# Two-layer transformer kernel: GpSimd normalises each item's second head, one sum for queries and keys, weight loads on SyncE's queue, a first swap by TensorE

## The reference, cut to what matters

```python
def _rope(x, sin, cos):
    xe = x[..., ::2]
    xo = x[..., 1::2]
    re = xe * c - xo * s
    ro = xe * s + xo * c
    return jnp.stack((re, ro), axis=-1).reshape(x.shape)

def _attn(xq, ctx, wq, wkv, wo, bo):
    q = _heads(xq @ wq)
    k, v = jnp.split(ctx @ wkv, 2, axis=-1)
    ...
    q = _rope(q, sq, cq)
    k = _rope(k, sk, ck)
    sim = jnp.einsum('bhnd,bhmd->bhnm', q, k) * DH ** (-0.5)
    a = jax.nn.softmax(sim, axis=-1)
    o = jnp.einsum('bhnm,bhmd->bhnd', a, v)
    ...
    return o @ wo + bo
```

## Time and profile before

| | |
|---|---|
| Time, median of 3 runs | 410.18 us (409.72 to 411.91) |
| Profiled execution | 409.6 us, span 407.5 us |
| PE / DVE / ACT / POOL busy in the span | 93% / 79% / 73% / 38% |
| Share of the chain that ended last: PE, ACT, DVE, issue, POOL | 22%, 8%, 6%, 5%, 2% |

### The profile page before, as it was taken

The page is one execution under the profiler, slowest core; times in us unless marked ns, Lnnn a source line. Parts: engine busy times, 40 slices in busy tenths (PEclk is TensorE's granted clock), DMA queues, the critical chain, the costliest instruction groups (busy, mean ns, idle before and its releaser), DMA issues. The chain is left out here.

```text
span 407.5 us, 9917 instructions
## 1 busy us (share of the span) xinstructions
PE 380.4 (93%) x3600; PEld 286.3 (70%) x3600; DVE 321.4 (79%) x700; ACT 297.8 (73%) x1033; POOL 153.9 (38%) x145
## 2 busy tenths in 40 slices
PE   7689998999989999999999898989899999999997
PEld 3456676776767877777777667775777777787664
DVE  4799999889898898998898857764658878888740
ACT  2367687787786786887878894679579787987832
POOL 4565445442652432634244425330246530202010
PEclk9989999999999999999999999999999999999999
DMA  6234524323324122122221110000000000000001
GB/s 215 90 117 138 187 86 155 130 82 129 104 74 185 53 80 79 53 77 80 80 77 66 72 47 27 2 2 1 2 2 2 2 2 3 2 2 2 2 0 51
DMA packets 15970, 26.08 MB, mean 64 GB/s; under 512 B 3598, under 2 KB 5908, under 8 KB 15796
## 3 DMA queue, kind: packets, MB, share of 16 engines
q1 hardware_dynamic: 13588, 18.49, 12.7%
q0 software_dynamic: 1616, 5.97, 4.9%
q10 hardware_dynamic: 720, 1.00, 0.8%
HBM read 8.15 MB, written 0.52 MB: 21 GB/s over the span
## 5 line engine op out<-in xcount | busy, mean ns | idle before, releaser
L284 POOL TENSOR_TENSOR swp<-swp,small 128x512 f32<-128x512 f32 x64 | 82.2, 1297 | 121.5 <-PE bank L917 77.2
L411 ACT ACTIVATE prob<-bank,nmax 128x128 f32<-128x128 f32 x256 | 91.2, 390 | 4.1 <-DVE nmax L693 4.1
L506 ACT ACTIVATE raw<-bank,nmax 128x128 f32<-128x128 f32 x256 | 72.7, 390 | 13.7 <-DVE nmax L799 13.4
L411 ACT ACTIVATION_READ_ACCUMULATOR prob<-bank,nmax 128x1 f32 x256 | 59.1, 231 | 0.0
L799 DVE TENSOR_REDUCE nmax<-bank 128x4 f32<-128x512 f32 x64 | 41.2, 684 | 17.8 <-PE bank L917 17.8
L693 DVE TENSOR_REDUCE nmax<-bank 128x4 f32<-128x512 f32 x64 | 41.2, 685 | 16.9 <-PE bank L917 16.9
L917 PE MATMUL bank<-hT,wqkv 128*128 128x512 f32 x96 | 49.9, 606 | 1.1 <-ACT hT L393 1.1
L700 DVE TENSOR_TENSOR prob<-prob,rz 128x512 f32<-128x512 f32 x64 | 48.7, 762 | 2.2
L417 ACT ACTIVATE probT<-bank 128x512 f32<-128x512 f32 x32 | 19.1, 597 | 40.3 <-PE bank L1004 40.3
L239 POOL TENSOR_TENSOR rstd<-vare,neg_half 128x4 f32<-128x4 f32 x12 | 12.4, 1032 | 95.0 <-DVE vare L628 94.9
L1004 PEld LDWEIGHTS bank<-small,prob 128*128 128x128 f32 x256 | 28.8, 140 | 26.3 <-DVE prob L700 15.0
(11 more groups left out here) (113 smaller groups left out, 643.3 us busy)
## 6 DMA issues: line engine op xcount, KB each, us to landing
swp<-raw SPq DMA_DIRECT2D x128, 128.0 KB, 2.1
wqkv<-in_wqkv POOLq DMA_DIRECT2D x13, 256.0 KB, 3.4
wff<-in_wff POOLq DMA_DIRECT2D x1, 1024.0 KB, 5.9
wsq<-in_wsq POOLq DMA_DIRECT2D x1, 576.0 KB, 5.8
x<-in_x SPq DMA_DIRECT2D x2, 256.0 KB, 4.6
wqkv<-in_wqkv ACTq DMA_DIRECT2D x2, 256.0 KB, 6.0
wmod<-in_wmod POOLq DMA_DIRECT2D x1, 512.0 KB, 4.2
ctx<-in_ctx SPq DMA_DIRECT2D x1, 384.0 KB, 7.2
```

What stands on the lines that cost most here:

```text
L284: nc.gpsimd.tensor_tensor(four(swp[:, m % 2, f, :]), four(swp[:, m % 2, f, :]), sin[f], ALU.mult).then_inc(rope_sin[f], 1)
L411: last = nc.scalar.activation(prob[:, hh, bcols(u)], S[hh][:, bcols(u)], ACT.Exp, bias=nmax[:, s % 2, hh, u:u + 1], accum_out=zsum[:, s % ...
L506: last = nc.scalar.activation(prob1[:, s % 2, hh, bcols(u)], score_bank(s, hh)[:, bcols(u)], ACT.Exp, bias=nmax[:, s % 2, hh, u:u + 1])
```

## The change

Five things change in layer 0, and some places in layer 1 are moved.

1. The second head's multiplication by the inverted row sums moves from VectorE to GpSimd (`normalise_second`). VectorE still inverts the sums (`invert_sums`).
2. `rope_sum` adds queries and keys in one instruction of 1024 elements and stands ahead of `normalise`. Its semaphore `roped` is one for both.
3. The weight loads move from GpSimd's queue to SyncE's, behind `swap(m)`, after a wait for the next score; the three large ones are cut in pieces.
4. Item 0 is not swapped by DMA: TensorE multiplies by weights whose columns are swapped in pairs already (`wswap`, a new 128 x 256 input), VectorE reads that product from S[0] and S[1] for the sine, and the programs' starts are reordered around it.
5. In slot 28 ScalarE's `scale_shift(2, 0)` stands between the two heads' exponentials; in slot 30 TensorE's `prob_values(29)` and VectorE's `ln_normalise` change place. In layer 1, `turn_back(0)` and `divide(0)` move from slot 5 to slot 8 and to bank Y, and ScalarE's `scale_shift(3, 1)` moves ahead of the second exponential of slot 6.

```diff
@@ SyncE
             def swap(m):
                 for f in range(2):
-                    sp.wait_ge(raw_out[f], m + 1)
+                    sp.wait_ge(raw_out[f], m)
...
+            sp.wait_ge(rope_sin[1], 1)
+            loads(0)
+            for m in range(2, ITEMS):
                 swap(m)
+                if m <= 22:
+                    sp.wait_ge(scores[0], m)
+                    loads(m - 1)
@@ GpSimd
+            def normalise_second(s):
+
+                pool.wait_ge(recips[1], s + 1)
+                nc.gpsimd.tensor_tensor(four(prob[:, 1, :]), four(prob[:, 1, :]),
+                                        rz[:, s % 2, 1, :].unsqueeze(2).broadcast_to([P, HALF, P]), ALU.mult).then_inc(
+                    norms[1], 1)
+
             def l0_slot(s):
+                if s >= 1 and s != 30:
+                    normalise_second(s - 1)
                 if 0 <= s < ITEMS - 2:
                     pool.wait_ge(scores[0], s + 1)
-                if s + 1 < ITEMS - 1:
+                if 1 <= s + 1 < ITEMS - 1:
                     rope_sine(s + 1, 0)
                     rope_sine(s + 1, 1)
-                loads(s)
                 background0(s)
@@ VectorE
+            def rope_sum(m):
+                for f in range(2):
+                    if m:
+                        dve.wait_ge(rope_sin[f], m)
+                    else:
+                        dve.wait_ge(first_sin[f], 1)
+                    dve.wait_ge(rope_cos[f], m + 1)
+                nc.vector.tensor_tensor(qk[:, m % 2, :, :], qk[:, m % 2, :, :], swp[:, m % 2, :, :], ALU.add).then_inc(
+                    roped, 1)
...
             def l0_slot(s):
-                if s >= 1:
-                    normalise(s - 1, 1)
-                if s >= 0:
-                    row_max(s, 0)
-                    row_max(s, 1)
+                row_max(s, 0)
+                row_max(s, 1)
                 if s + 1 < ITEMS - 1:
                     rope_cosine(s + 1, 1)
                 middle0(s)
                 if s >= 1:
                     copy_T0(s - 1)
-                if s >= 0:
-                    normalise(s, 0)
...
                 shift0(s)
                 if s + 1 < ITEMS:
-                    rope_sum(s + 1, 0)
-                    rope_sum(s + 1, 1)
+                    rope_sum(s + 1)
+                normalise(s)
+                invert_sums(s, 1)
                 if s + 2 < ITEMS:
                     rope_cosine(s + 2, 0)
                 background0(s)
@@ TensorE
+            def first_fills():
+                wait_hT(0, 0)
+                pe.wait_ge(ld_wqkv[0], 16)
+                pe.wait_ge(ld_swap, 16)
+                fill_swapped(1)
+                fill(0, 1)
+                fill_swapped(0)
+                fill(0, 0)
+                fill(0, 2)
+                fill(1, 0)
+                fill(1, 1)
...
             def turn_back(g):
                 pe.wait_ge(os_out, g + 1)
                 if g == 0:
-                    pe.wait_ge(gelu_done, FF + 2)
+                    pe.wait_ge(proj_out, AT["q", 1] + 1)
```

More of the change, by code:

```diff
@@ L62, in copied_by_act, with swaps, build @@
     return s < RUN or s % RUN in (0, 2, 4)
-def build(nc, small_in, x_in, ctx_in, ctxT_in, wqkv_in, wmod_in, wsq_in, wff_in, row_in, out):
+def swaps(m):
+    return (m + 1) // 2
+def build(nc, small_in, x_in, ctx_in, ctxT_in, wqkv_in, wswap_in, wmod_in, wsq_in, wff_in, row_in, out):
     es = ExitStack()
@@ L352, in _ @@
             pool.wait_ge(ld_tab, 16)
-            for s in range(-1, ITEMS):
+            for s in range(ITEMS):
                 l0_slot(s)
+            normalise_second(ITEMS - 1)
             for j in range(1, SLOTS):
@@ L460, in l0_slot @@
             def l0_slot(s):
[L461 to L465, removed]
                 if s >= 2:
@@ L597, in _ @@
             scale_shift(0, 0, T[0])
-            for s in range(-2, ITEMS):
+            evacuate_v(0)
+            evacuate_raw(1, 0)
+            evacuate_raw(1, 1)
+            for s in range(ITEMS):
                 l0_slot(s)
@@ L848, in middle1 @@
                     ln_normalise(3, 1)
+                if s == RUN:
+                    divide(0)
                 for run in range(3):
@@ L906, in _ @@
             dve.wait_ge(ld_tab, 16)
-            rope_cosine(0, 0)
-            for s in range(-1, ITEMS):
+            first_rope(1)
+            first_rope(0)
+            rope_sum(0)
+            context_stats(0)
+            context_stats(1)
+            rope_cosine(1, 0)
+            for s in range(ITEMS):
                 l0_slot(s)
@@ L979, in score @@
             def score(s):
[L980 to L983, removed]
+                pe.wait_ge(roped, s + 1)
+                if s:
+                    for hh in range(2):
+                        pe.wait_ge(exps[hh], s)
                 if s == 29:
@@ L1093, in down, with fill_swapped @@
                     last.then_inc(acc_done[half], 1)
+            def fill_swapped(f):
+                mm(S[f][:, :], wswap[:, f * P:(f + 1) * P], hT[:, 0, :], True, True).then_inc(first_swap[f], 1)
+            def first_fills():
[9 more added lines that the diff above has]
+                fill(1, 1)
             def l0_slot(s):
[L1096 to L1099, removed]
                 score(s)
+                if s == 0:
+                    fill(1, 2)
                 if s >= 1:
@@ L1106, in l0_slot @@
                     project_out(s - 2)
+                if s == 30:
+                    prob_values(29)
                 if s != 29:
                     background0(s)
-                if s + 2 < ITEMS:
+                if s == 0:
+                    fill(2, 1)
+                    fill(2, 2)
+                elif s + 2 < ITEMS:
                     fill(s + 2, 2)
@@ L1268, in l1_slot @@
                     project("k", 1)
+                if s == RUN:
+                    turn_back(0)
                 if s in (2 * RUN - 1, 3 * RUN - 1):
@@ L1284, in background1 @@
                     e = RUN * run
-                    if s == e + (8 if run else 5):
+                    if run and s == e + 8:
                         turn_back(2 * run)
@@ L1349, in _ @@
             pe.wait_ge(mod_read, 1)
-            for s in range(-2, ITEMS):
+            first_fills()
+            for s in range(ITEMS):
                 l0_slot(s)
```

125 lines of the change are left out of this document (66 added, 59 removed).

## The result

The changed kernel takes 423.69 us (median, 423.38 to 424.07) against 410.38 beside it: ratio 1.032, 95% interval 1.029 to 1.035, + 13.3 us. The profiled execution took 423.91, span 422.1 against 407.5. The forecast was 417.5 with a range to 422.0: the way and the loop came out, the size did not.

What follows compares the result with a forecast made beforehand. TensorE's own work sets a plain slot; the new order closes a loop of 7.50 us. + 9.7 - 2.2 + 0.6 - 0.4 = + 7.7 on 409.6 gives 417.3, forecast 417.5, range 411 to 422.

Steps and rivals of the forecast that it cites:

- the loop: Layer 0 slots: score, sines, sum, first head's multiplication, transposes, next score; 7.53 us, used as 7.50; chance 0.69.
- the 215.7 of my sum: Layer 0 slots 0 to 27: 28 x 7.50 = 210.0 plus 2.7, 2.5 and 0.5 for longer slots; 205.98 before.
- semaphore to VectorE: 0.06: Link from the sines' end to the sum, estimated from the 0.05 between VectorE's multiplication and TensorE's transposes.
- Sum to inversion: Link for the one sum of 1024 elements on VectorE: taken as 1.14 us, between 1.03 and 1.21.
- The swap's landing: Layer 0 slots: swapped keys land at 9.4, ahead of the second sine at 10.0, so the DMA costs nothing.
- a rival with the weight loads as its cause (427): Weight loads hold up swaps, 0.5 for 20 slots, + 10; chance 0.08, shared with a late GpSimd multiplication.
- 4, 13 and 21: Layer 0 slots with `shift0` ahead of the sum, which starts at 4.7 instead of 3.8: + 0.9 each, 2.7.
- Hidden work: GpSimd's second head's multiplication, taken as 1.3 us, ends at 7.3 in the slot and costs nothing up to about 2.5.
- the two engines' overlap: VectorE's multiplication overlapping a GpSimd sine took 1.17 instead of 0.69; new order runs it while GpSimd is idle.
- Start and end: First score 2.2 earlier; slot 28's MLP product 0.6 later; layer 1 net - 0.4 from slots 5 and 8.
- The faster rival: Sines don't close the loop, VectorE's relief removes nearly all TensorE's 7.9 us idle in slots 0 to 27: 399.7; chance 0.12.

Runs made afterwards that it cites:

- experiment 1: Kernel before, with VectorE's two rope sums ahead of the first head's multiplication and nothing else changed: 425.16 us against 409.92.
- experiment 2: Changed kernel, with VectorE's first head's multiplication ahead of the one rope sum, as before the change: 405.36 us against 409.92 for the kernel before.
- experiment 3: Changed kernel, with GpSimd's sines no longer waiting for the slot's score: 420.89 us against 409.92 for the kernel before.
- 6: Changed kernel, with two rope sums of 512 instead of one of 1024, semaphore on the second: 418.63 us against 409.55 for the kernel before.
- experiment 5: Changed kernel, with SyncE's weight loads issued only after the slot's swapped keys have landed: 422.80 us against 409.55 for the kernel before.

## Why the prediction was right in kind and short in size

**The loop.** Right, and shown by undoing it on both sides: the order alone makes the kernel before as slow (1), the old order takes 17.9 us off the changed one (2). Its path was right for the changed kernel only: the sines set the sum's start by 0.35 over VectorE's own way (3.94 against 3.59), and without them the order would still have made a loop of about 7.3 (experiments 1, 3 and 6). The prediction had the two at 3.8 and 3.7 and treated the sines as what closes the loop. Slots 0 to 27 took 223.67 instead of the 215.7 of my sum, the first score to that of slot 28:

```profile
16.47 1.16 PE L956 MATMUL bank<-qk 64*128 64x128 f32 x16
...
240.14 1.05 PE L956 MATMUL bank<-qk 64*128 64x128 f32 x14
```

**The steps that failed.** Two terms of the sum were mis-sized.

- "semaphore to VectorE: 0.06". It was 0.20: I took VectorE to TensorE for GpSimd to VectorE. Sum to inversion, 1.15, was 1.14 in the text. The loop is 7.65; and I had rounded my own 7.53 down to 7.50. In the 20 slots that the sum set at 7.50, 0.15 is 3.0 of the missing 8.0.
- The swap's landing, "9.4" in the slot against a second sine at "10.0", which made the DMA cost nothing. That is raw keys to landing in 2.8. It holds in the slots without an instruction packet beside the swap (2.6), so the way of adding it up was right; in slots 3, 5, 7, 9 and 11 it was 4.3, 4.1, 3.4, 3.8 and 3.9. These slots exceed 7.65 by 0.88, 0.75, 0.64, 1.00 and 0.80, 4.1 in all. The fill of the keys is no cause by itself: in slots 7 and 9 they were out 0.38 before the score, half a microsecond later than forecast, but 2.6 from there would still be ahead of the second sine at 2.46. I had late swaps only as a rival with the weight loads as its cause (427); without the loads the five slots take as long (experiment 5).

The rest is 0.7 in slots 0 and 1, where item 1's swap starts late, and 0.4 in slots 17, 23 and 25, which have such a packet too, less 0.3 in 4, 13 and 21, which took 8.31 rather than 8.4. With the two steps that makes 7.9 of the 8.0.

**Hidden work.** Right. GpSimd's multiplication takes 1.04, under the 1.3 that I took, and no TensorE wait names it in the changed kernel. All 32 are alike in the source view (ns, min/median/max):

```profile
L335 POOL TENSOR_TENSOR prob<-prob,rz x32: 1037/1041/1044, 24.0 to 276.1; 128x512 f32<-128x512 f32 x32
L730 DVE TENSOR_TENSOR prob<-prob,rz x32: 691/691/736, 23.2 to 274.0; 128x512 f32<-128x512 f32 x32
```

The second row also agrees with what the prediction said of the two engines' overlap: in the new order VectorE's multiplication overlaps no sine. 29 of the 32 overlap nothing on GpSimd and took 0.69; three ran beside its layernorm scaling and took 0.74. In experiment 2, where it stands ahead of the sum again, ten overlap a sine and took between 0.69 and 1.27, so an overlap does not stretch it every time.

**Start and end.** The first score came 2.52 earlier, forecast 2.2. From slot 28's score to the end it took 0.6 less, where I had 0.2 more: slots 28 to 31 cost 0.24 instead of 0.6, and layer 1 gained 0.8 instead of 0.4 (slot 5 took 5.58 instead of 7.41, slot 8 4.38 instead of 3.60).

**The faster rival.** Its condition was met by experiment 2, yet it gave 405.4 and not 399.7. The step that fails is that TensorE's 7.9 us of idle time goes once VectorE is relieved. It doesn't go even with 21 us less work on VectorE: 7.75 remain. A part is named by waits: in slot 13 of experiment 2, 8.89 long, `prob_values` waits for ScalarE's hT:

```profile
118.89 1.09 PE L956 MATMUL bank<-probT,v 128*64 128x128 f32 x16 [1.05 <-ACT hT L417]
```

and late swaps hold other slots. The score that ends slot 1 (7.86 long) waits 0.88 for the sum; there the first sine waited 2.26 for the DMA and the second ended 6.4 into the slot. In slot 5 (7.34) the second sine waited 1.54 for the DMA. How much of the 7.75 late swaps make up in all was not tested.

## What to carry to other kernels

Before moving an instruction ahead of another on an in-order engine, walk from it around to itself: if the path goes through another engine's wait for this slot's own first result, the move closes a loop, and every latency on it is paid in every slot. There can be more than one such path: here taking GpSimd's out (experiment 3) gave 0.35 of the 1.00, because VectorE's own was nearly as long. Relieving an engine that is 90% busy gained 1 us at most here, since a second engine set the pace. When a transfer's slack is small, look at the spread of its landing over the slots and not only at its median. Merging two instructions saves a fixed part, but makes the first half wait for the second half's input.

## What the runs showed of the hardware that was not expected

- A float32 multiplication of 128 x 512 by a factor that repeats along the row took 1.04 us on GpSimd, the one by a table of 128 columns 1.26 or 1.27.
- GpSimd's end to VectorE's start took 0.20 in this loop, VectorE's end to TensorE's start 0.05.
- A swap of 2 x 64 partitions x 2 KB, issued as two DMAs, landed 2.58 to 2.62 us after the first issue in 14 slots of the changed kernel, and 3.06 to 4.26 in the 12 in which a 16 KB instruction packet moved meanwhile. That the packet causes it is inferred.
- After TensorE had waited 2.03 us in slot 7 of experiment 1, its granted clock was 0.50 over the next 3.0 us (79.7 to 82.7).
